# Expert row stores from GpSimd's queue to non-overlapping result rows, and a changed order of the first products

## The reference, cut to what matters

```
xn  = layernorm(x)                        # x: 1024 tokens x 256
out = x + attention(xn) + ffn(xn)

attention:  q, k, v = split(xn @ w_qkv);  q = elu(q)+1;  k = elu(k)+1       # 16 heads of 16
            skv_t = decay * skv_(t-1) + k_t * v_t      # causal scan over the tokens
            sk_t  = decay * sk_(t-1) + k_t
            return (q * skv / max(sum over a head of q * sk, 1e-6)) @ w_out

ffn:        expert = argmax(xn @ router_w.T)           # one of 8 for each token
            gate   = sigmoid(largest logit)
            routed = silu_mul((xn*gate) @ w_gate_up[expert]) @ w_down[expert]   # 256 -> 2x512 -> 256
            shared = silu_mul(xn @ shared_gate_up) @ shared_down                # 256 -> 2x512 -> 256
            return routed + shared
```

## Time and profile before

| | |
|---|---|
| median of 3 runs | 128.49 us (128.0 to 129.37) |
| the profiled execution | 127.59 us |
| its span, from the first instruction to the last | 125.8 us |
| PE busy | 117.3 us (93%) |
| DVE, ACT, POOL busy | 81.9, 47.1, 28.3 us |
| granted TensorE clock | 1.00 |

### The profile page before, as it was taken

How to read it: one execution, slowest core, us unless ns; L and a number is a source line. 1 busy time by engine, 2 the same in 40 slices (tenths; PEclk the granted TensorE clock), 3 DMA queues, 4 the chain that set the end, 5 groups by cost and what they waited for, 6 DMA issues and landing times.

```text
span 125.8 us, 2452 instructions
## 1 busy us (share of the span) xinstructions
PE 117.3 (93%) x759; PEld 100.9 (80%) x759; DVE 81.9 (65%) x182; ACT 47.1 (37%) x93; POOL 28.3 (23%) x51
## 2 busy tenths in 40 slices
PE   4989999999999999999999999897969999999970
PEld 1258776788888857999999998896969979999970
DVE  0799695999969987777839392937050547913371
ACT  1578796827987646312020202220110209100000
POOL 7804040029878300000000000000000000687500
PEclk9999999999999999999999999999999999999999
DMA  3683999999999238735999999977933243133427
GB/s 101 195 277 47 303 327 233 187 169 297 386 403 348 90 68 360 194 53 138 351 228 381 200 352 268 345 201 238 325 66 57 52 76 67 29 96 89 120 96 246
DMA packets 25804, 25.35 MB, mean 201 GB/s; under 512 B 14264, under 2 KB 24000, under 8 KB 24768
## 3 DMA queue, kind: packets, MB, share of 16 engines
q1 hardware_dynamic: 23760, 22.22, 61.9%
q0 software_dynamic: 768, 2.10, 5.1%
q10 hardware_dynamic: 1264, 0.88, 2.3%
HBM read 18.95 MB, written 6.24 MB: 200 GB/s over the span
## 4 chain that ended last, share of the span: by engine, by line
PE 35%; DMA 21%; SPq 19%; issue 10%; POOL 5%; DVE 4%; ACT 3%; DVEq 0%; ACTq 0%; POOLq 0%
DMA sorted_rows<-yrow 11%; SPq L314 8%; SPq L354 6%; PE ps L303 5%; POOL q_sb L468 5%; PE ps L304 5%; PE ps L305 5%; PE ps L1102 5%; DMA wqkv<-in_L_attn_w_qkv_dram 4%; PE ps L997 3%; PE ps L990 3%; PE ps L984 3%; DMA x_sb<-in_L_attn_x_dram 2%; DMA q_sb<-sorted_rows,slot_row 2%; PE ps L1111 2%
## 5 line engine op out<-in xcount | busy, mean ns | idle before, releaser
L1102 PE MATMUL ps<-xgT,gu 128*128 128x144 f32 x192 | 24.5, 286 | 0.0
L1102 PEld LDWEIGHTS ps<-xgT,gu 128*128 128x128 f32 x192 | 24.0, 190 | 0.1
L468 POOL DMA_INDIRECT q_sb<-sorted_rows,slot_row x8 | 8.3, 1039 | 67.7 <-DMA sorted_rows<-yrow 65.6
L579 ACT ACTIVATE rz<-ps 128x144 f32<-128x144 f32 (+1 forms) x24 | 7.9, 330 | 37.1 <-PE ps L1102 37.1
L823 DVE STREAM_TRANSPOSE yrow<-ps 128x320 f32<-128x320 f32 x8 | 4.1, 515 | 19.3 <-DMA sorted_rows<-yrow 19.3
L1111 PE MATMUL ps<-wqkv,dn 128*128 128x144 f32 x96 | 13.0, 289 | 1.7 <-DVE wqkv L828 1.7
L1111 PEld LDWEIGHTS ps<-wqkv,dn 128*128 128x128 f32 x96 | 12.2, 196 | 2.1 <-DVE wqkv L828 2.1
L303 PE MATMUL ps<-xT_hi,sgu_hi 128*128 128x512 f32 x32 | 12.9, 402 | 0.0
L304 PE MATMUL ps<-xT_lo,sgu_hi 128*128 128x512 f32 x32 | 12.6, 395 | 0.0
L305 PE MATMUL ps<-xT_hi,sgu_lo 128*128 128x512 f32 x32 | 12.6, 394 | 0.0
L460 POOL DMA_INDIRECT sorted_rows<-xn,slot_row x8 | 9.1, 1143 | 2.3 <-issue 2.3
(11 more groups left out here) (156 smaller groups left out, 219.2 us busy)
## 6 DMA issues: line engine op xcount, KB each, us to landing
gu<-in_L_ffn_w_gate_up_dram SPq DMA_DIRECT2D x6, 1024.0 KB
dn<-in_L_ffn_w_down_dram SPq DMA_DIRECT2D x6, 512.0 KB
sorted_rows<-zeros SPq DMA_DIRECT2D x1, 2608.0 KB, 19.8
xT_raw<-in_L_ffn_w_gate_up_dram SPq DMA_DIRECT2D x2, 1024.0 KB, 5.0
wqkv<-sorted_rows SPq DMA_DIRECT2D x40, 40.0 KB, 2.7
sorted_rows<-yrow SPq DMA_DIRECT2D x34, 40.0 KB, 3.7
sgu<-_ffn_shared_gate_up_dram SPq DMA_DIRECT2D x1, 1024.0 KB, 6.0
ez<-in_L_ffn_w_down_dram SPq DMA_DIRECT2D x2, 512.0 KB, 6.3
```

The source lines that it names most:

```text
L468: pool.indirect_dma_start(y_tok[:, i, :], None, sorted_rows, bass.IndirectOffsetOnAxis(ap=slot_row[:, i:i + 1], axis=0)).then_inc(s_gather ...
L579: A(silu_part(h), ps[:, GATE[h], 0:len(PARTS[h]) * SLOTS], ACT.Silu).then_inc(s_silu, 1)
L1102: ins = mm(ps[:, (GATE, UP)[u][h], j * SLOTS:(j + 1) * SLOTS], gu_of[p][:, kc, col:col + P], xgT[:, kc, 0:SLOTS], start=(kc == 0), stop=(k ...
```

## The change

- The row stores of all tiles but the last go from SP's to POOL's queue. `yrow` has three buffers: results 1 to 6 alternate between the first two, the loop uses the third, the last result the second. Each has its semaphore. POOL in the loop waits for its four stores to land before it frees the buffer.
- Result t (1, 2, ...) goes to rows 160 (t - 1) and on, so that no store overlaps another. Where a token's result lies is no longer its slot row: DVE computes it (`done_row`) with four small instructions after `head_reciprocals(3)`, from the slot and a table `bounds` that POOL makes at the start. POOL's gathers use it.
- The first store (of a cleared `yrow`) and the clearing are gone.
- At the end SP stores its half of the last result ahead of its wait for the last load.
- `WARM` is 12 rather than 14. Tile 0 of the query, key and value products runs high and low weights by the first 128 channels, then the same by the second. DVE takes all four statistics of the second half after the splits, instead of two before them. The second half's tokens are transposed inside tile 4 instead of tile 3. ACT copies the head table after the weights' high parts instead of ahead of the tokens'.

On PE the router and head tables stood ahead of the token transposes before as well.

```diff
-WARM = 14
+WARM = 12
...
-        yrow = sb("yrow", [P, NSQ, SQ * KC], F32)
+        yrow = sb("yrow", [P, 3, NSQ, SQ * KC], F32)
...
-        def row_store(eng, t, q, s_store):
+        def row_store(eng, t, b, q, s_store):
-            rows = sorted_rows[bass.ds(t * SLOTS, NSQ * SQ), q * SQ * KC:(q + 1) * SQ * KC]
-            eng.dma_start(rows.rearrange("(j p) f -> p j f", p=SQ), yrow[q * SQ:(q + 1) * SQ, :, :]).then_inc(s_store, 16)
+            rows = sorted_rows[bass.ds(t * (NSQ * SQ) - NSQ * SQ, NSQ * SQ), q * SQ * KC:(q + 1) * SQ * KC]
+            eng.dma_start(rows.rearrange("(j p) f -> p j f", p=SQ), yrow[q * SQ:(q + 1) * SQ, b, :, :]).then_inc(s_store, 16)
...
                 with sp.Fori(ends[e - 1] if e else 0, ends[e]) as t:
-                    sp.wait_ge(s_yrow, t + 1)
-                    for q in range(P // SQ):
-                        row_store(sp, t, q, s_ystore)
                     sp.wait_ge(s_xgc, t + 2)
                     sorted_load(t * SLOTS + 3 * SLOTS, s_xg)
...
-            sp.wait_ge(s_xg, 64 * ends[7] + 64)
             sp.wait_ge(s_lastrow, 1)
             for q in range(2):
-                row_store(sp, ends[7], q, s_ylast_sp)
+                row_store(sp, ends[7], 1, q, s_ylast_sp)
+            sp.wait_ge(s_xg, 64 * ends[7] + 64)
...
+            pool.wait_ge(s_plan, 1)
+            total = pool.value_load(plan[0:1, E - 1:E], min_val=E, max_val=TILES)
+            for t in range(1, E - 1):
+                pool.wait_ge(s_yrow, t + 1)
+                for q in range(P // SQ):
+                    row_store(pool, t, (t - 1) % 2, q, s_ystore[(t - 1) % 2])
+            with pool.Fori(E - 1, total) as t:
+                pool.wait_ge(s_yrow, t + 1)
+                for q in range(P // SQ):
+                    row_store(pool, t, 2, q, s_yloop)
+                pool.wait_ge(s_yloop, 64 * t - 64 * (E - 2))
+                pool.sem_inc(s_yfree, 1)
+            for b in range(2):
+                pool.wait_ge(s_ystore[b], 64 * ((E - 1 - b) // 2))
             pool.wait_ge(s_qkv_sum, KC)
+            pool.wait_ge(s_done_row, 1)
...
             for i in range(NT):
                 pool.indirect_dma_start(y_tok[:, i, :], None, sorted_rows,
-                                        bass.IndirectOffsetOnAxis(ap=slot_row[:, i:i + 1], axis=0)).then_inc(s_gather[i], 16)
+                                        bass.IndirectOffsetOnAxis(ap=done_row[:, i:i + 1], axis=0)).then_inc(s_gather[i], 16)
...
-            act.wait_ge(s_hrow, 1)
-            A(head_row[:, :], ps[:, HROW, 0:P], ACT.Copy).then_inc(s_hrowc, 1)
             x_hi(0)
...
+            act.wait_ge(s_hrow, 1)
+            A(head_row[:, :], ps[:, HROW, 0:P], ACT.Copy).then_inc(s_hrowc, 1)
...
-            for i in range(TH, TH + 2):
-                statistics(i)
             x_lo(0)
             dve.wait_ge(s_whv, 1)
             w_lo(2).then_inc(s_wlv, 1)
-            for i in range(TH + 2, NT):
+            for i in range(TH, NT):
                 ins = statistics(i)
...
+            def first_tile(t):
+                if t >= 3:
+                    dve.wait_ge(s_ystore[(t - 1) % 2], 64 * ((t - 1) // 2))
+                if t:
+                    rows_out(t, (t - 1) % 2, s_yrow)
+                expert_tile(t)
...
             head_reciprocals(3)
+            dve.wait_ge(s_bounds, 2)
+            link(V.tensor_tensor(past[:, :, :], slot[:, :].unsqueeze(2).broadcast_to([P, NT, TILES - 1]),
+                                 bounds[:, :].unsqueeze(1).broadcast_to([P, NT, TILES - 1]), ALU.is_ge))
+            link(V.tensor_reduce(tile_at[:, :], past[:, :, :], AX.X, ALU.add))
+            link(V.scalar_tensor_tensor(done_at[:, :], tile_at[:, :], float(NSQ * SQ - SLOTS), slot[:, :], ALU.mult, ALU.add))
+            V.tensor_copy(done_row[:, :], done_at[:, :]).then_inc(s_done_row, 1)
...
             with dve.Fori(E - 1, total) as t:
+                dve.wait_ge(s_yfree, t - (E - 2))
+                rows_out(t, 2, s_yrow)
                 expert_tile(t)
-            rows_out(total, s_lastrow)
+            dve.wait_ge(s_ystore[1], 64 * ((E - 2) // 2))
+            rows_out(total, 1, s_lastrow)
...
-                hi_hi()
-                if t == 3:
-                    transpose_tokens(1)
                 if t == 0:
-                    lo_hi(False)
+                    pe.wait_ge(s_wlk, 1)
+                    for kc in range(KC):
+                        pe.wait_ge(s_xhi, kc + 1)
+                        mm(o, wqkv_hi[:, kc, cols], xT_hi[:, kc, rows], start=(kc == 0), stop=False)
+                        mm(o, wqkv_lo[:, kc, cols], xT_hi[:, kc, rows], start=False, stop=False)
                     ins = hi_lo(True)
                 else:
+                    hi_hi()
+                    if t == 4:
+                        transpose_tokens(1)
                     hi_lo(False)
```

More of the change, by code:

```diff
@@ L108, in build @@
         slot_row = sb("slot_row", [P, NT], I32)
+        bounds_int = sb("bounds_int", [P, TILES - 1], I32)
+        bounds = sb("bounds", [P, TILES - 1], F32)
+        past = sb("past", [P, NT, TILES - 1], F32)
+        tile_at = sb("tile_at", [P, NT], F32)
+        done_at = sb("done_at", [P, NT], F32)
+        done_row = sb("done_row", [P, NT], I32)
         plan = sb("plan", [1, E], I32)
@@ L269, in build @@
         s_yrow = sem("s_yrow")
-        s_ystore = sem("s_ystore")
+        s_ystore = [sem(f"s_ystore{b}") for b in range(2)]
+        s_yloop = sem("s_yloop")
+        s_yfree = sem("s_yfree")
+        s_bounds = sem("s_bounds")
+        s_done_row = sem("s_done_row")
         s_lastrow = sem("s_lastrow")
@@ L430, in _ @@
             pool.memset(ones8[:, :], 1.0).then_inc(s_const, 1)
-            pool.memset(yrow[:, :, :], 0.0).then_inc(s_yrow, 1)
+            pool.sem_inc(s_yrow, 1)
+            pool.sem_inc(s_yfree, 1)
+            pool.iota(bounds_int[:, :], pattern=[[SLOTS, TILES - 1]], base=SLOTS, channel_multiplier=0).then_inc(s_bounds, 1)
+            pool.wait_ge(s_bounds, 1)
+            pool.tensor_copy(bounds[:, :], bounds_int[:, :]).then_inc(s_bounds, 1)
             pool.wait_ge(s_const, 15)
@@ L599, in _ @@
             for q in range(2, P // SQ):
-                row_store(act, total, q, s_ylast_act)
+                row_store(act, total, 1, q, s_ylast_act)
             attention_hi(0)
@@ L817, in _, with rows_out @@
             hidden_lo(LAST - 1)
-            def rows_out(t, s_done):
+            def rows_out(t, b, s_done):
                 dve.wait_ge(s_down, t)
-                dve.wait_ge(s_ystore, 64 * t)
-                V.transpose(yrow[:, :, :].rearrange("p j (f c) -> p c j f", c=KC), ps[:, 5:7, 0:NSQ * SQ]).then_inc(s_done, 1)
+                V.transpose(yrow[:, b, :, :].rearrange("p j (f c) -> p c j f", c=KC), ps[:, 5:7, 0:NSQ * SQ]).then_inc(s_done, 1)
             def expert_part(t, h):
@@ L829, in expert_part, with expert_tile @@
                                 ps[:, UP[h], 0:width * SLOTS], ALU.mult).then_inc(s_hr, 1)
-            def expert_tile(t, first=False):
-                if not first:
-                    rows_out(t, s_yrow)
+            def expert_tile(t):
                 expert_part(t, 0)
@@ L855, in attention_lo @@
                 V.tensor_tensor(att_lo[:, c, cols], kvsum[:, c, cols], att_hi[:, c, cols].bitcast(F32), ALU.subtract).then_inc(s_attl, 1)
-            expert_tile(0, first=True)
+            def first_tile(t):
[4 more added lines that the diff above has]
+                expert_tile(t)
+            first_tile(0)
             dve.wait_ge(s_denc, 1)
@@ L861, in _ @@
             kv_scan(1)
-            expert_tile(1)
+            first_tile(1)
             kv_scan(2)
             kv_scan(3)
-            expert_tile(2)
+            first_tile(2)
             head_reciprocals(0)
@@ L868, in _ @@
             V.tensor_tensor(sdn_lo, sdn[:, :, :], sdn_hi.bitcast(F32), ALU.subtract).then_inc(s_plo, 1)
-            expert_tile(3)
+            first_tile(3)
             head_reciprocals(1)
@@ L875, in _ @@
             V.tensor_tensor(wout_lo, wout[:, :, :], wout_hi.bitcast(F32), ALU.subtract).then_inc(s_plo, 1)
-            expert_tile(4)
+            first_tile(4)
             head_reciprocals(3)
+            dve.wait_ge(s_bounds, 2)
[4 more added lines that the diff above has]
+            V.tensor_copy(done_row[:, :], done_at[:, :]).then_inc(s_done_row, 1)
             for c in range(KC):
@@ L880, in _ @@
                 V.tensor_tensor(kvsum[:, c, :], q_sb[:, c, :], kvsum[:, c, :], ALU.mult).then_inc(s_qkv_sum, 1)
-            expert_tile(5)
+            first_tile(5)
             dve.wait_ge(s_rhigh, 1)
             V.scalar_tensor_tensor(rden_split, rden, low_row[:, 0:1], rden_hi.bitcast(F32), ALU.mult, ALU.add).then_inc(s_rsplit, 1)
-            expert_tile(6)
+            first_tile(6)
             with dve.Fori(E - 1, total) as t:
+                dve.wait_ge(s_yfree, t - (E - 2))
+                rows_out(t, 2, s_yrow)
                 expert_tile(t)
```

(5 more changed lines are left out.)

1 line of the change is left out of this document (added).

## The result

The kernel after takes 124.28 us (median of 4 runs, 124.09 to 124.46). Beside it the kernel before took 128.25 us (126.94 to 129.37). The ratio is 0.9745, 95% interval 0.9694 to 0.9797: faster by 2.5%, in the range forecast, but less than the 5.0 us forecast. The profiled execution took 124.46 us, its span is 122.8 us against 125.8, so 3.0 us less from trace to trace; the medians are 4.0 us apart.

A forecast was written before the change was run, and what follows sets the result against it. PE, 93% busy, was taken to lose 3.9 us in expert tiles to DVE's waits for stores. Start 0.6, tiles 3.6 and end 0.8 make 5.0 us: 123.5 on the median's scale; 8-in-10 range 121.8 to 127.2.

The forecast's parts named there:

- The cause named: Expert tiles: DVE's result transposes wait 19.3 us for earlier stores to land, delaying down products; PE loses 3.9 us.
- the start: Shorter warming, reordered tile 0 and later second token transposes: together 0.6 us sooner, bounds 0.8 and -0.5.
- the end: After the last expert tile: gathers start sooner, PE's chain then sets the end; 0.8 us gained, bounds 0.3 and 1.1.
- SP's queue at nothing: SP without 32 stores of some 0.5 us: loads and weights come a little earlier, never later; priced at nothing.
- the 3.6 us forecast for the expert tiles: Eight expert tiles: 3.9 us of PE's delays removed, less 0.3 for `done_row`, 3.6 us sooner.
- rival (b): Expert tiles: DMA transfers stay the limit, stores and loads land as late, only start and end gain: 127.1; chance 0.09.
- The prediction's own sign of being wrong: Expert tiles: one of its signs was a period still above 6.3 us with loads or weights named in the waits.
- POOL's stores: Expert tiles: 1.4 us a store, 5.6 a tile, hidden behind the tile; priced from POOL's indirect transfers.
- Rival (a): POOL's stores slow, gathers queue behind them; break-even 1.73 a store, far end 129.7; slower by over 1%: chance 0.12.
- `done_row`: Tile 4: four small DVE instructions, about 1.0 us, charged 0.3 us to PE, bounds 0 and 1.0.
- the middle term: The expert tiles' part of the sum: 3.6 us sooner.
- lower bound of 121.8: Whole kernel: low end of the range for 8 in 10, all bounds of the gains together.

The follow-up runs named there:

- one buffer's wait: Kernel after, stores on POOL, but each result transpose waits until the store just before it has landed: 129.02 us, 1.003 to the kernel before.
- The start alone: Kernel before with only the start of the kernel after: 126.46 us, 0.9954 to the kernel before.

## Why the prediction was right, and where it was not

*The cause named was right.* DVE's waits for stores went (19.3 us to none), and with them the delays of PE after them. Both parts of the change are needed. With one buffer's wait the gain is gone by the ratio, and half of what tiles 1 to 7 gained is gone in the quickest execution. With three buffers but SP's stores the gain is 1.4%, no more than the start and the end account for.

*The step that failed* is the one that put SP's queue at nothing: "SP keeps the loads ... loads and weight loads come a little earlier, never later. At nothing, covered by the products." They had no cover. Before, DVE's waits for stores had hidden that the tokens are hardly in time (its token transposes waited 1.0 us for them in all). At PE's own pace they are late enough to hold PE in tiles 2 and 5, by 0.6 and 0.9 us, since each expert's 1.5 MB of weights has to pass in the same 5.9 us. The third late tile, tile 0, has another cause: PE's pace was the same there before (5.87). Expert 2's weights were issued 1.9 us later than before and met the token loads: the last scatter began 0.8 us later in that execution, and SP took 1.0 us longer to issue the first token loads. So of the 3.6 us forecast for the expert tiles 1.3 came: 49.63 us (49.82 to 99.45) against 50.97. Tiles 1 to 7 gave 2.4, and tile 0 took 1.0 back. Without the down weights the stage takes 47.1, so the size of the stall that could be removed was right, 3.8 us, and 2.5 of it turned into another wait. That trace had a short tile 0, as its scatters ended early, so 1.5 of the 2.5 are the down weights'. It was rival (b), with a chance of 0.09, that came true in part: not that landing stays as late for all, but for those loads that meet weights. That the engines were "90% busy or more in seven slices on end" stood in the text and was given too little weight: a stage made 8% shorter needs 8% more from the engines that carry it.

The prediction's own sign of being wrong was a period above 6.3 us with loads named in the waits; it came out at 6.24 (first products from 49.82 to 93.48 over seven tiles), with the loads named.

*POOL's stores* were priced at 1.4 us each, 5.6 a tile. The tile view after (duration ns min/median/max):

```profile
L324 POOL DMA_DIRECT2D sorted_rows<-yrow x28: 573/573/674, 59.5 to 96.9; - x28
```

They take 0.573 each and four of them 2.3 us a tile. Rival (a) is out, by a factor of three from its break-even of 1.73. The nearest row, an indirect transfer, was a poor measure for a direct one: it costs half, pauses included even less. The rule of the Trainium skill on GpSimd's descriptors and VectorE's two-port mode (SBUF — State Buffer, "SBUF: two separate sides") gives 3100 ns for the case it describes; no store here took over 0.67 us. Whether VectorE was in that mode beside any of them, no run shows, so this neither confirms nor refutes the rule. They are issued fast but land late, in the DMA issues of the page (count, KB each, median us to landing):

```profile
wqkv<-sorted_rows SPq DMA_DIRECT2D x40, 40.0 KB, 2.9
sorted_rows<-yrow POOLq DMA_DIRECT2D x28, 40.0 KB, 5.1
```

5.1 us where SP's stores took 3.7. That fits into the two tiles that the buffers give, as forecast, and not into one: with one buffer's wait DVE waited 12.3 us for stores.

*`done_row`* was priced at 1.0 us of DVE and 0.3 us for PE. It takes 0.83 us of DVE's time from its first instruction to the products behind it:

```profile
80.63 0.21 DVE L907 TENSOR_TENSOR past<-slot,bounds 128x112 f32<-128x112 f32 x1
...
80.88 0.27 DVE L909 TENSOR_REDUCE tile_at<-past 128x8 f32<-128x112 f32 x1
81.18 0.17 DVE L910 SCALAR_TENSOR_TENSOR done_at<-tile_at,slot 128x8 f32<-128x8 f32 x1
81.38 0.17 DVE L911 CAST done_row<-done_at 128x8 int32<-128x8 f32 x1
81.46 2.35 DVE L914 TENSOR_TENSOR kvsum<-q_sb,kvsum 128x1024 f32<-128x1024 f32 x2
```

and costs PE nothing: without down weights the tile after it begins 5.89 us after the one before.

*The start* was forecast at 0.6. First products begin at 8.69 instead of 8.97, tile 0 of the experts at 49.82 instead of 50.30: 0.5. The start alone gives 0.5%. In the kernel after it could not be told from nothing: tile 0's wait for tokens took it back.

*The end* was forecast at 0.8 and gave 1.2: from the last expert tile to the span's end 23.35 us against 24.53. It went as described. From the timeline after (compare):

```profile
100.51 1.22 SPq L324 DMA_DIRECT2D sorted_rows<-yrow  x2
...
104.14 1.04 POOL L494 DMA_INDIRECT q_sb<-sorted_rows,done_row  x1 [6.67 <-DMA sorted_rows<-yrow]
...
119.55 0.42 DVE L941 TENSOR_TENSOR x_sb<-x_sb,ps 128x256 f32<-128x256 f32 x1 [0.30 <-PE ps L315]
120.26 0.42 DVE L941 TENSOR_TENSOR x_sb<-x_sb,ps 128x256 f32<-128x256 f32 x1 [0.29 <-PE ps L315]
```

The gathers begin 4.7 us after the last tile (3.7 forecast, 6.6 before; SP's two stores began 0.3 us later than forecast and took 1.22 us to issue instead of 0.86) and still have time to spare: DVE's last additions wait for PE, so that PE sets the end.

*Sum:* 0.5 + 1.3 + 1.2 = 3.0 us from trace to trace, where 0.6 + 3.6 + 0.8 = 5.0 was forecast. The miss lies in the middle term, and 1.0 us of it in a tile whose length changed with the execution. The medians differ by 4.0 us. One slip in the prediction's working: its lower bound of 121.8 is 127.59 less 5.8, the profiled execution's scale; on the median's scale, which the forecast uses, it is 122.7. The result lies above both.

## What to carry to other kernels

When a wait is taken off an engine, list what else has to be there at the new pace and how many bytes must pass in the shorter stage; a transfer that was just in time under a stall is late without it. The order of issue on one queue can be a throttle that helps: a small urgent load is best issued when no bulk transfer has just been started. A bulk transfer whose buffers are free early can be issued early, ahead of a long wait in the same program, but look first whether the DMA engines are idle there, and what small transfers are then under way. Here the row of an indirect transfer overstated a direct one by half and more: such a row bounds a price and does not give it. And look at one stretch in several traces before a microsecond of it is put down to a change.

## What the runs showed of the hardware

- Weights under way delay a small transfer: four loads of 40 KB landed in 1.7 to 1.9 us after issue with no weights under way, in 3.8 to 4.5 with 1.5 MB under way, and in 2.0 to 3.0 with 1 MB.
- A queue of its own does not protect a small transfer: 40 KB loads of 256-byte pieces on ACT's queue were waited for 10.5 us in all, on SP's, behind and ahead of the weights, 6.7. The Trainium skill, DMA: Bandwidth & Descriptors, "Issuing engines are not separate DMA queues", says that transfers of all queues run on the same 16 engines and interleave; these runs agree.
- Whether tile 0 waits for its tokens changes with how late the scatters end, by little more than a microsecond. Expert 2's weights were issued at 45.01, 45.25 and 45.61 us in three traces (the start alone, the run without down weights, the kernel before), and DVE did not wait for the token loads issued at 48.6 to 49.2; in six traces, at 46.55, 46.57, 46.58, 47.28, 47.50 and 47.96, it waited 1.80, 1.54, 1.04, 1.66, 1.78 and 2.07. The run without down weights is the same kernel as after up to that place, so it is the execution and not the code that differs between these two. The clearing of the table is 2.6 MB; it took 19.4 us to land in the run without down weights and 20.4 in the kernel after. In all six traces POOL's first scatter waited for it, by 0.54 to 1.11 us, and in the three others it did not. That its landing is what varies was read from the traces and not tested. Nor is it known whether the change makes the late landing more frequent: both traces with the old stores are among the three.
- POOL's direct stores of 160 pieces took 0.573 us each, its indirect gathers of 128 rows 0.94 at the least, in the same kernel.
